# Gates on GpSimd, two output rows on TensorE and moved steps in an attention and Sinkhorn kernel

## What is computed

```
# 1: windowed attention on layernorm(x), windows of W = 128 columns, 8 heads of 32
q = einsum('ed,bdw->bew', Wq, patches(LN(x))) + bq      # k the same, v from ctx
scores = einsum('bhdi,bhdj->bhij', qh, kh) / sqrt(32);  masked; attn = softmax(scores)
o = gelu(einsum('bhij,bhdj->bhdi', attn, vh));  out = einsum('de,bew->bdw', Wo, o) + bo
x = x + tanh(g_xattn) * out * masks
# 2: on layernorm(x), each row of 2048 read as n = 4 streams of C = 512
logits = x_norm @ [W_res, W_pre, W_post].T + bases      # x_norm: RMS norm
H_res = sinkhorn_log(logits_res, num_iters=50, tau=0.1) # 4 x 4 for each row
H_pre, H_post = softmax(...), softmax(...)
H_res = (1 - g) * I + g * H_res
y = einsum('btnc,btn->btc', x_streams, H_pre) @ W_branch
ffn = einsum('btij,btjc->btic', H_res, x_streams) + einsum('btc,btn->btnc', y, H_post)
x = x + tanh(g_ffn) * ffn
```

## Time and profile before

| | us |
|---|---|
| median of 3 runs | 1790.07 |
| lowest, highest | 1785.03, 1795.5 |
| the profiled execution | 1789.35 |
| its span in the trace | 1787.5 |
| DVE busy | 1303.3 (73%) |
| PE busy | 1411.3 (79%) |
| ACT busy | 1133.5 (63%) |
| POOL busy | 808.1 (45%) |

### The profile page before, as it was taken

How to read it: one execution, slowest core, us unless ns; L and a number is a source line. 1 busy time by engine, 2 the same in 40 slices (tenths; PEclk the granted TensorE clock), 3 DMA queues, 4 the chain that set the end, 5 groups by cost and what they waited for, 6 DMA issues and landing times.

```text
span 1787.5 us, 36543 instructions
## 1 busy us (share of the span) xinstructions
PE 1411.3 (79%) x12736; PEld 882.2 (49%) x12736; DVE 1303.3 (73%) x3542; ACT 1133.5 (63%) x2305; POOL 808.1 (45%) x1373
## 2 busy tenths in 40 slices
PE   2679999988898888888888889888888897435335
PEld 0455566555555555554555455555555564224224
DVE  3244343566778888888788888887788878768988
ACT  2457878777677776777667767777777765322212
POOL 3323335355645564556555564556465634440000
PEclk9689999999999999999999999999999998657768
DMA  8456776666667766676676767676666554412123
GB/s 254 133 150 183 200 191 192 164 192 171 185 179 197 194 189 188 185 202 182 182 203 184 199 170 203 178 202 173 176 181 182 154 132 105 127 63 82 71 71 141
DMA packets 175462, 299.93 MB, mean 168 GB/s; under 512 B 25104, under 2 KB 76176, under 8 KB 171184
## 3 DMA queue, kind: packets, MB, share of 16 engines
q1 hardware_dynamic: 157872, 264.04, 48.9%
q0 software_dynamic: 17408, 33.56, 10.8%
HBM read 179.81 MB, written 67.11 MB: 138 GB/s over the span
## 4 chain that ended last, share of the span: by engine, by line
DVE 30%; PE 26%; ACT 14%; POOL 13%; issue 12%; SPq 3%; DMA 2%; DVEq 0%; POOLq 0%; ACTq 0%
PE pr L685 9%; PE pr L699 7%; POOL kp L575 7%; DVE ssum L1276 5%; ACT squares L971 3%; DVE sv L1277 3%; DVE otile_even L1305 3%; DVE xpre L1293 2%; POOL x1c L510 2%; DVE sa L1277 2%; DVE otile_odd L1305 2%; DVE otile_even L1321 2%; DVE x1c L1172 2%; PE av_ps L816 2%; DVE negm L1154 2%
## 5 line engine op out<-in xcount | busy, mean ns | idle before, releaser
L575 POOL TENSOR_TENSOR kp<-ke,sv 128x64 f32<-128x64 f32 x329 | 149.1, 453 | 282.9 <-DVE sv L1277 282.2
L1276 DVE TENSOR_REDUCE ssum<-kp 128x16 f32<-128x64 f32 x768 | 182.5, 238 | 123.5 <-POOL kp L575 116.7
L491 POOL TENSOR_TENSOR x_hl<-xc,x_hl 128x512 bf16<-128x512 f32 x128 | 156.3, 1221 | 153.3 <-ACT x_hl L899 153.3
L699 PE MATMUL pr<-wv,ctx_hl 128*128 128x256 bf16 x1536 | 195.7, 289 | 26.2 <-DVE k_hl L1139 20.2
L1162 DVE TENSOR_TENSOR o_sb<-av_ps,rden 128x128 f32<-128x128 f32 x256 | 72.8, 284 | 192.3 <-ACT rden L940 188.7
L575 POOL TENSOR_TENSOR kp<-ke,sa 128x64 f32<-128x64 f32 x343 | 149.4, 435 | 139.8 <-DVE sa L1277 139.8
L685 PE MATMUL pr<-x_hl,wq 128*128 128x512 bf16 x768 | 182.8, 389 | 35.3 <-POOL x_hl L491 35.3
L816 PE MATMUL av_ps<-probs,v_t 128*32 128x128 f32 x2048 | 111.6, 289 | 122.1 <-DVE o_sb L1162 121.7
L685 PE MATMUL pr<-x_hl,wk 128*128 128x512 bf16 x768 | 206.0, 426 | 0.0
L1154 DVE TENSOR_REDUCE negm<-s_ps 128x4 bf16<-128x512 f32 x256 | 166.8, 651 | 48.9 <-PE s_ps L789 48.2
L931 ACT ACTIVATE probs<-st_ps,key_bias 128x512 f32<-128x512 f32 x256 | 173.4, 677 | 37.3 <-PE st_ps L803 37.0
(11 more groups left out here) (157 smaller groups left out, 3055.5 us busy)
## 6 DMA issues: line engine op xcount, KB each, us to landing
xs<-in_dram SPq DMA_DIRECT2D x128, 256.0 KB, 5.8
xc<-in_dram SPq DMA_DIRECT2D x128, 256.0 KB, 4.3
ctx_raw<-in_dram SPq DMA_DIRECT2D x32, 1024.0 KB, 7.7
x1c<-in_dram POOLq DMA_DIRECT2D x64, 512.0 KB, 7.6
x_dram<-x1c SPq DMA_DIRECT2D x32, 1024.0 KB, 5.1
q_st<-q_hl SPq DMA_DIRECT2D x384, 64.0 KB
k_st<-k_hl SPq DMA_DIRECT2D x384, 64.0 KB
x1t_even<-x_dram SPq DMA_DIRECT2D x16, 1024.0 KB, 5.9
```

Source lines behind the costliest of these rows:

```text
L491: nc.gpsimd.tensor_tensor(x_hl[:, G % 2, 1, t, :], xc[:, t, :], x_hl[:, G % 2, 0, t, :], ALU.subtract).then_inc(x_split, 1)
L575: nc.gpsimd.tensor_tensor(kp[:], ke[:], v, ALU.mult).then_inc(kp_made, 1)
L699: ins = nc.tensor.matmul(bank(what)[:, j * E:(j + 1) * E], ctx_hl[:, a, t, win], wv[:, m, t, :], start=(t == 0 and a + m == 0), stop=(t == ...
L1276: cf.link(nc.vector.tensor_reduce(s_t, k, AX.X, ALU.add))
```

## The change

1. **ACT's order.** `squares` and `inverse_roots` come ahead of the bank copies in a step, and the fourth square moves from r = 4 to r = 5, with the norms behind it one step later.
2. **Tiles of f up to 5** (BESIDE). Everything but load, the first product, xpre and the copies for it comes one step later. So y (four instructions on DVE) comes into the step that has xpre (three).
3. **Tiles of f = 6** (AMID, new). Rows 2 and 3 are made by PE as four fp32 products of 128 x 512 with diagonals (`mix_row`), for which ACT makes eight diagonals and reads two rows back (`diagonals_row`, `read_row`) in place of two first products; DVE has 10 instructions per tile instead of 16, with y last.
4. **Gates.** In steps without Sinkhorn, POOL waits for `max_done` of the step ahead of its early part and for `o_done` ahead of its late part.
5. **Norms on POOL.** Both `moments` go into the late part of u = 13, `scale_b` into u = 15 (late) and 16, and `norm_b` into u = 17 (late), behind the coefficients.
6. **Head.** The column sums of the logits' weights (`csum`, 32 matmuls) go from step -1 to step -2, and the second context's load from r = 4 to r = 5, behind the copies of k.

```diff
-SQUARES_AT = [3, 4, 4, 4]
+SQUARES_AT = [3, 4, 4, 5]
...
-BESIDE = dict(load=-8, first=-6, xpre=-5, pre=-3, branch_0=0, branch_1=1, out_0=-1, out_1=0,
+BESIDE = dict(load=-9, first=-7, xpre=-6, pre=-4, branch_0=0, branch_1=1, out_0=-1, out_1=0,
               stream_1=0, stream_2=1, y=2, stream_3=4, pair_1=5, pair_2=6, pair_3=7, store_0=5, store_1=8)
...
+AMID = dict(load=-5, diag=-3, mix=-2, branch_0=-1, branch_1=-1, diag_2=-2, diag_3=-1, row_2=-1, row_3=0,
+            out_0=-1, read_2=0, read_3=1, stream_1=0, stream_2=1, stream_3=2, y=3, store_0=4, store_1=5)
...
-TILE_AT = {(f, t): UNITS * (f + 1) + 54 + UPC * t for f in range(LAST_BESIDE + 1) for t in range(DT)}
+TILE_AT = {(f, t): UNITS * (f + 1) + 55 + UPC * t for f in range(LAST_BESIDE + 1) for t in range(DT)}
...
-    if g == -1:
+    if g == -2:
         made.append(("csum", 0, 0))
...
-                if r == 4 and 1 <= G + 2 < NG:
+                if r == (4 if G >= 0 else 5) and 1 <= G + 2 < NG:
                     sp.wait_ge(ctx_split, G + 2)
                     load_ctx(G + 2)
...
+                if its == (None, None) and 2 <= g < NU:
+                    pool.wait_ge(max_done, g + 1)
 
                 low = at_step(g, -1, LOW_CTX_AT)
...
-                for ready in ffn_at(g, STAT_AT + 1):
-                    moments(ready, 0)
-                for ready in ffn_at(g, STAT_AT + 2):
-                    scale_b(ready, 0)
+                for ready in ffn_at(g, STAT_AT + 3):
+                    scale_b(ready, 1)
                 scale_at(f, its, 2)
+                if its == (None, None) and 2 <= g < NU:
+                    pool.wait_ge(o_done, g - 1)
...
-                for ready in ffn_at(g, STAT_AT + 1):
+                for ready in ffn_at(g, STAT_AT):
+                    moments(ready, 0)
                     moments(ready, 1)
                 for ready in ffn_at(g, STAT_AT + 2):
-                    scale_b(ready, 1)
+                    scale_b(ready, 0)
                 for ready in ffn_at(g, STAT_AT + 4):
                     norm_b(ready)
...
+            def mix_row(f, t, i):
+
+                n, m = DT * f + t, 2 * t + i - 2
+                row = (s_ps, st_ps)[i % 2]
...
+                for j in range(N):
+                    ins = nc.tensor.matmul(row[:], diag_r[:, i % 2, j, :], x1t[n % 2][:, j * C:(j + 1) * C],
+                                           start=(j == 0), stop=(j == N - 1))
+                ins.then_inc(row_full, 1)
...
+            def read_row(f, t, i):
+                act.wait_ge(row_full, 2 * t + i - 1)
+                nc.scalar.activation(otile[(DT * f + t) % 2][:, i, :], (s_ps, st_ps)[i % 2][:], ACT.Identity,
+                                     bias=ccon[:, f % 2, t, i:i + 1]).then_inc(acc_ready, 1)
...
+                for i in (2, 3):
+                    for done, t in tiles_at(g, f"read_{i}"):
+                        read_row(done, t, i)
+                for n, at in enumerate((STAT_AT + 1, STAT_AT + 4)):
+                    for ready in ffn_at(g, at):
+                        inverse_roots(ready, n)
...
+                for H, t in at_step(g, 2, SQUARES_AT):
+                    square_x1(H, t)
                 made = banked_at(g)
...
-                    if j == N - 1:
+                    if j == N - 1 and f != B - 2:
                         ins.then_inc(out_ready, 1)
...
+                if last:
+
+                    nc.vector.memset(spare[:, 1:2], 0.0).then_inc(out_ready, 1)
```

## The result

The changed kernel takes 1803.18 us (median of 6 runs, 1800.32 to 1804.11), the kernel before 1791.64 beside it; the ratio is 1.0056, with a 95% interval of 1.0035 to 1.0077. It is slower by about 10 us, where I had forecast 20 us less and a range that ended at 1793. Its profiled execution has a span of 1802.3.

A forecast was written before the change was run, and what follows sets the result against it. No engine is full: PE paces early chunks, DVE the Sinkhorn-and-tile chunks and the end. Head -5.3, early chunks -1, middle -7.4, tail -6 sum to -19.7 against 1789.35: 1770 us, 8-in-10 range 1748 to 1793.

The forecast's parts named there:

- The step that failed: Middle, r = 1 and 2: steadier PE leaves idle under 1, k bank at 2.75 instead of 4.45, so -1.7 us.
- I had -0.1: Middle, chunks u = 24 to 31 and 8 to 15: +1.6 for r = 0 and 1, -1.7 behind, -0.1 us each.
- +1.6 booked for r = 0 and 1: Middle: y joins xpre in r = 1, r = 0 gives back only part, so both together +1.6 us a chunk.
- rival (a): Middle: y's place makes r = 1 alone longer, +2.6 in 21 chunks, +55, about 1825; chance 0.12 for anything above 1798.
- Squares: Middle, r = 5: DVE's reciprocal wait shrinks little, PE's transposed scores ending 0.3 behind; -0.6 us a sequence (-3 to 0).
- Gates: Steps without Sinkhorn: logit instructions no longer blocked by POOL's splits, -3.2 us; L1305 pairs in other steps -0.7 a sequence.
- Norms: u = 13: moments wait for the late square and DVE behind them, +2.0; scale_b in u = 15 +0.5; +2.5 us a sequence.
- Head: Before the first scores: column sums hidden in PE's wait, 7.0 gained, 1.7 lost to the later context load; -5.3 us.
- Behind the attention: Last Sinkhorn: 24 fewer DVE instructions -13.7, links +0.8, later ke +5, norm_b +1, moments +1; -6 us (-13 to +2).
- The lock: r = 0: stream_2 and POOL's DMA issue might exclude each other on a shared port, +25 in 21 chunks, 1795; chance 0.03.

The follow-up runs named there:

- run 2: The kernel before with only its output tiles of f up to 5 one step later (y beside xpre in r = 1): 1843.04 us, ratio 1.0268.
- run 8: The kernel before with only the squares ahead of ACT's bank copies, each in its old step: 1750.37 us, ratio 0.9756.
- run 4: The changed kernel with the fourth square back in r = 4 and the norms in their old steps and order: 1781.86 us, ratio 0.9921.
- run 11: The changed kernel with the tiles of f = 6 as before, all four rows by DVE and ACT: 1810.03 us, ratio 1.0097.
- run 9: The changed kernel with the tiles of f up to 5 in their old steps and the norms in their old order: 1716.68 us, ratio 0.9555.
- run 3: The changed kernel with xpre alone one step later, in r = 2, apart from y: 1725.99 us, ratio 0.9619.
- run 7: The kernel before with only the two gates on POOL: 1770.99 us, ratio 0.9866.

## Why the prediction was wrong

**The two harmful parts against each other.** All in one table, in us (medians of several comparisons; those of the kernel before lie between 1791.5 and 1797.7), with squares, gates, head and f = 6's rows in each:

| | norms new | norms old |
|---|---|---|
| y and xpre in r = 1 (as changed) | 1803 | 1782 |
| tiles back | 1773 | 1717 |
| xpre in r = 2 | 1726 | 1713 |

Each undone alone gives 21 and 30, both 86. The two single runs scatter by some 20 us, but even their quickest executions (1767 and 1765) together give less, 74. In the profiled executions the old place of the norms is worth 50 us with the tiles back and 15 with the tiles as changed. One part of this I can read, in the step u = 18. With tiles back and norms old it lasts 6.6 us in most sequences: the gates hold the splits off. With tiles back and norms new it lasts 9.1 to 10.4 in four of seven, with this in the timeline of PE and ACT:

```profile
661.18 0.66 PE L843 MATMUL av_ps<-probs,v_t 128*32 128x128 f32 x8 [2.40 <-DVE o_sb L1215]
...
666.04 5.33 PE L696 MATMUL pr<-x_hl,wq 128*128 128x512 bf16 x12
...
671.40 0.69 ACT L943 ACTIVATE q_hl<-pr,bq_sb 128x512 bf16<-128x512 f32 x1 [8.13 <-PE pr L696]
```

PE idles 2.40 in u = 16, falls to half clock, needs 5.33 for a q bank, and ACT waits 8.13 for that. With y in r = 1, on the other hand, u = 17 lasts 7.0 in place of 4.3, and u = 18 only 4.7; as I read it, the late scale of the norms and the splits hide there. So one loss covered part of the other, and where I priced each by itself, on the rows of before, I could not see it. But u = 18 makes only 8 of the 35 us between 50 and 15. The rest is spread over other steps, u = 12, 16 and 20 to 22 most, and its cause stays open.

Point by point:

- **The step that failed** is "With PE fed more steadily in r = 1, the idle should fall to under 1 and the bank to 2.75: -1.7." The opposite came: DVE's division comes 2.5 us later in its step, and the branch's second part, which PE now makes first, covers only some 1.5 of them (PE's busy time in r = 1 is 6.14 against 4.60). The idle is 2.8 to 3.6, and in the chunks shown either the k bank of r = 2 (4.35) or the v bank of r = 4 (5.30) runs at half clock. Together r = 0 to 4 got 1 to 4 us longer in 18 of 21 chunks and 0 to 0.3 in the other three, which hold the softmax step; I had -0.1. The crowded step itself I had about right: +1.6 booked for r = 0 and 1, +1.8 measured. The rival (a) named the place and nearly the size, +55 for 21 chunks against 48 alone (run 2), but not the way, and that its size fits is in part luck: in run 2 r = 1 costs 58, r = 0 and 2 give back 41, 22 of them in the softmax steps, and r = 3 and 4 cost 32 more. I gave it 0.12 because I summed DVE's work over three steps, as if PE could use what r = 0 and 2 gave back.
- **Squares** were mis-sized most: -0.6 for a sequence, -3 in all, against -41 (run 8). I took the next bound, PE's transposed scores 0.3 behind, for fixed. It was not: PE's idle time in the middle fell by 21 us and its busy time by 14, DVE's waits for the reciprocal by 37 (188.7 to 151.8). As I read it PE, which itself waits for DVE's earlier divisions, moved along with them; no run shows this link by itself.
- **Gates**: -3.2 for the logits and -0.7 for the other steps of a sequence, about -21 in all, was booked; -24 alone, 19 within the change. Right in mechanism and size, though in the step shown L1272 takes 1.54 and not 0.8.
- **Norms**: +2.5 a sequence; 3 in the changed kernel (run 4), and DVE's wait of 2.64 in u = 13 as forecast. Right there, but 56 us beside the old tiles, which nothing in my sum told.
- **Head**: -5.3; the first maximum is 8.5 earlier, that of step 8 4.6. Right; the second chunk's longer wait for k was not foreseen.
- **Behind the attention**: -6 booked, -5.0 measured from the last maximum to the end. Against run 11 its parts were right one by one: `ke` +5.0 (I had +5), the Sinkhorn -14.0 (-12.9). But even in run 11 `ke` comes 3.1 later than in the kernel before (108.2 against 105.1), for which I had 2 by the norms; run 4, with the norms back, gives back 0.8 of it.
- **The lock** of rows 5: loads and POOL's DMA issues did nothing that the timelines show; the issue at 856.73 takes 1.24, as before.

So with squares at -41, gates at -24, f = 6 at -7 and the head at -5, the change had 77 us to gain by the single runs, and run 9, which has these four together, gained 81; the norms and the place of y ate all of it and 10 more. My two large errors had opposite signs, so that the total was off by only 33 us: luck, and it hid how little I knew of either.

The granted clock of the middle goes with the waits: 0.95 before, 0.93 in the changed kernel and in run 2, 0.96 in runs 3 and 8. (Over the whole span it is 0.91 before and 0.915 changed, for behind the attention, where PE has more to do, it rose from 0.69 to 0.77.) The Trainium skill, "TensorE: Matmul & The Clock Gate", Part 1, has an idle PE fall to 1.2 GHz until it has been busy for some time. The rows agree, though not for each idle: 12 matmuls take 4.35 behind an idle of 2.94, but 2.76, as at full clock, behind one of 2.81. So where it happens a wait of 2.94 costs 1.6 more in the bank behind it.

## What to carry to other kernels

Two engines that wait for each other once a step did not trade work between steps here: the fullest step of the slower one counted, not the sum over three, and an idle of TensorE of 2 to 3 us was often followed by a bank at half clock. The order in one engine's queue can be worth more than the work itself: an instruction that is ready (a square here) belongs ahead of one that still waits for another engine (the copy of a bank), so that it does not push back what others wait for (the reciprocal). That gave 41 us by moving nothing but places. And undo a change's parts alone and in pairs: 21 and 30 us made 86.

## What the runs showed of the hardware

A DVE instruction of 128 x 32 took 0.99 us in the mean of four beside GpSimd's 128 x 512 splits; with the gates (run 7) the mean of all 32 fell from 0.805 to 0.321 us, and the median is 0.24; holding GpSimd back by two semaphores in 95 steps, with no work removed, was worth 24 us. An idle of 1.84 to 2.94 us on PE was followed now by a bank at full clock (a k bank of 2.76 behind 2.81, a v bank of 2.79 behind 1.84), now by one at half (a k bank of 4.35 behind 2.94, a v bank of 5.30 behind 1.85); what decides between the two these runs don't settle.
